# First batch of the attention projected, split and stored during the last scans; mask rows made by GpSimd at the start

## What is computed

```python
x = _layernorm(x + _L0_attn_ref(x, ...))       # state-space layer with a scan over positions
x = _layernorm(x + _L0_xattn_ref(x, ctx_2048, mask, mask, Wq, bq, Wk, bk, Wv, bv))
x = _layernorm(x + _L0_ffn_ref(x, w_gate_up, w_down))

# in _L0_xattn_ref: 16 heads of 16 channels; 512 queries and 512 keys for each of 16 batches
q = einsum('oc,bct->bot', Wq, target) + bq     # k and v likewise, from ctx
dot = einsum('bhdt,bhds->bhts', q, k) / sqrt(16)
m = mask_t * mask_s
dot = m * dot - (1.0 - m) * 1e6
out = einsum('bhts,bhds->bhdt', softmax(dot) * m, v)
```

## Time and profile before

| | us |
|---|---|
| median of 3 runs (lowest, highest) | 3583.75 (3581.31, 3584.29) |
| the profiled execution | 3582.23 |
| its span, first to last instruction | 3580.4 |

### The profile page before, as it was taken

The page is one execution under the profiler, slowest core; times in us unless marked ns, Lnnn a source line. Parts: engine busy times, 40 slices in busy tenths (PEclk is TensorE's granted clock), DMA queues, the critical chain, the costliest instruction groups (busy, mean ns, idle before and its releaser), DMA issues. The chain is left out here.

```text
span 3580.4 us, 53813 instructions
## 1 busy us (share of the span) xinstructions
PE 3088.7 (86%) x16101; PEld 1821.8 (51%) x16134; DVE 2916.8 (81%) x2901; ACT 2561.1 (72%) x4966; POOL 2256.2 (63%) x1409
## 2 busy tenths in 40 slices
PE   8788888888888888898887479899899899969998
PEld 5566656656666666566655233343343343324444
DVE  6999989989989989889999477677777777548886
ACT  6888877878878778788876137566666666757776
POOL 4999999989999999999999224233333334300000
PEclk9999999999999999999998689999999999989999
DMA  4102210210122022202210445554554555231110
GB/s 156 59 8 74 72 57 23 74 69 25 56 74 70 7 75 71 69 11 74 72 57 27 119 141 152 158 162 149 163 165 146 163 167 149 73 114 48 41 47 33
DMA packets 163681, 310.68 MB, mean 87 GB/s; under 512 B 22544, under 2 KB 80016, under 8 KB 163296
## 3 DMA queue, kind: packets, MB, share of 16 engines
q1 hardware_dynamic: 159088, 299.46, 26.4%
q10 hardware_dynamic: 4352, 8.39, 0.9%
HBM read 216.11 MB, written 91.69 MB: 86 GB/s over the span
## 5 line engine op out<-in xcount | busy, mean ns | idle before, releaser
L737 POOL TENSOR_TENSOR bu<-du,bc 128x1024 f32<-128x1024 f32 x512 | 1196.7, 2362 | 90.6 <-DVE dt L329 45.1
L810 DVE TENSOR_TENSOR_SCAN states<-states,bu 128x1024 f32<-128x1024 f32 x448 | 1026.6, 2292 | 118.5 <-ACT states L662 73.8
L662 ACT ACTIVATE states<-dt,negA 128x256 f32<-128x256 f32 x2048 | 851.0, 462 | 356.8 <-DVE hc L823 307.2
L1460 DVE TENSOR_REDUCE mmax<-s_ps 128x2 f32<-128x1024 f32 x512 | 624.8, 1224 | 285.0 <-PE s_ps L1180 270.8
L1296 ACT ACTIVATE pt<-s_ps 128x512 f32<-128x512 f32 x1024 | 572.7, 596 | 319.2 <-PE s_ps L1189 308.0
L484 PE MATMUL y_ps<-id_sb,hc 128*128 128x128 f32 x3584 | 485.9, 280 | 156.4 <-DVE hc L823 156.3
L823 DVE TENSOR_TENSOR hc<-states,bc 128x1024 f32<-128x1024 f32 x448 | 548.6, 1225 | 47.0 <-DVE states L810 1.9
L484 PEld LDWEIGHTS y_ps<-id_sb,hc 128*128 128x128 f32 x3584 | 410.7, 143 | 320.1 <-DVE hc L823 282.8
L1189 PE MATMUL s_ps<-qst,kst 105*128 105x512 bf16 x1024 | 380.6, 387 | 11.7 <-ACT pt L1296 5.1
L1180 PE MATMUL s_ps<-kst,qst 102*128 102x512 bf16 x1024 | 319.4, 395 | 54.7 <-DMA kst<-mask_d 44.8
L1200 PE MATMUL pv_ps<-pt,vaug 128*32 128x512 f32 x2048 | 278.4, 617 | 41.6 <-ACT o_sb L1331 41.5
(11 more groups left out here) (172 smaller groups left out, 4722.3 us busy)
## 6 DMA issues: line engine op xcount, KB each, us to landing
bc<-bc_scratch SPq DMA_DIRECT2D x128, 512.0 KB, 5.2
stack_d<-parts SPq DMA_DIRECT2D x192, 256.0 KB, 3.0
qst<-stack_d SPq DMA_DIRECT2D x64, 384.0 KB
kst<-stack_d SPq DMA_DIRECT2D x64, 384.0 KB
x<-xres SPq DMA_DIRECT2D x31, 512.0 KB, 6.2
w_raw<-in_w_ffn SPq DMA_DIRECT2D x48, 256.0 KB, 2.7
w_raw<-in_w_ffn SPq DMA_DIRECT2D x16, 768.0 KB, 6.8
xT_sb<-in_xT SPq DMA_DIRECT2D x16, 512.0 KB, 3.6
```

Source lines behind the costliest of these rows:

```text
L662: a = act.activation(states[:, bank, first:first + SEQ], dt[:, t, :], ACT.Exp, scale=negA[:, t, c * NS + n:c * NS + n + 1])
L737: pool.tensor_tensor(bu[:, buf, :].rearrange("p (n l) -> p n l", n=NS), du[:, t % (2 * GRP):t % (2 * GRP) + 1, :].to_broadcast([P, NS, SEQ ...
L810: m = dve.tensor_tensor_scan(dst, src, bu[:, BU_OF[k][0], half * 2 * SEQ:(half + n) * 2 * SEQ], 0.0, ALU.mult, ALU.add)
L1460: dve.tensor_reduce(mmax[:, u // HG, c:c + 2], s1_ps[:, pair], AX.X, ALU.max).then_inc(s1_free, 1)
```

## The change

The projections, split and stores of the attention's batch 0 move into the first stage's last batch (batch 15). SyncE loads their inputs, 1.79 MB in six DMAs, into tiles that the last batch no longer needs (`load_first_rows`, in batch 14 between the B and the C rows of batch 15). ACT takes the normalisation's sums (step 6) and scales (step 10), POOL its power (step 12); PE projects in steps 9, 11, 13 and 15, DVE masks in steps 10, 12, 14 and 16, ACT rounds in steps 15, 19, 19 and 23, POOL subtracts in steps 18, 21, 22 and 25; SyncE stores behind its loop (`store_first_rows`). One half output projection moves from step 14 to step 18, since it uses the bank. The mask rows are made by POOL at the program's start and stored before the first B and C rows. The second stage begins with body -1. SyncE issues only the loads of `qst`, `kst`, x and the mask there; ACT issues those of the parameters; the preset of `kst` is cut in two, and only its first half is waited for ahead of the first scores. Counts of semaphores are shifted by one batch to match; those lines are left out.

```diff
-            14: ((0, 0, 0, 2), (0, 1, 0, 2)), 20: ((0, 0, 2, 4), (0, 1, 2, 4)), 30: ((0, 0, 4, 6), (0, 1, 4, 6))}
+            14: ((0, 1, 0, 2),), 18: ((0, 0, 0, 2),), 20: ((0, 0, 2, 4), (0, 1, 2, 4)), 30: ((0, 0, 4, 6), (0, 1, 4, 6))}
 LAST_ADD = {7: 0, 11: 1}
+
+
+ROWS_AT = {("k", 0): (9, 10), ("k", 1): (11, 12), ("q", 0): (13, 14), ("q", 1): (15, 16)}
+NORM_AT, NORM_POW, NORM_END = 6, 12, 10
+CAST_AT = {("k", 0): 15, ("k", 1): 19, ("q", 0): 19, ("q", 1): 23}
+REST_AT = {("k", 0): 18, ("k", 1): 22, ("q", 0): 21, ("q", 1): 25}
...
+        a_wk, a_wq = [in_w(i * HID, HID).rearrange("p (k o) -> p k o", k=SEQT) for i in range(2)]
+        a_ctx, a_x, a_d, a_n, a_kf, a_qf = [in_w((i + 1) * 2 * HID, 2 * HID).rearrange("p (k t) -> p k t", k=SEQT) for i in range(6)]
+        a_m, a_m4 = [in_w(14 * HID + i * HID, HID) for i in range(2)]
...
+            sp.dma_start(mk, mask).then_inc(mk_in, 16)
...
+            sp.wait_ge(mk_ready, 1)
+            sp.dma_start(mask_d.rearrange("(b k) -> b k", b=BATCH), mk_rows.rearrange("b o r t -> b (o r t)")).then_inc(mk_out, 16)
...
+            def load_first_rows():
+                for kind in "scg":
+                    sp.wait_ge(mm[kind], BATCH * PER[kind])
+                sp.dma_start(a_x, x1[0].rearrange("(i p) h -> p i h", p=P)).then_inc(a_x_in, 16)
+                first = ctxt[0:SEQ * HID].rearrange("(i p h) -> p i h", p=P, h=HID)
+                for dst, src in ((a_ctx, first), (a_wk, wk), (a_wq, wq), (a_qkb, chan_qk), (a_m, mask[0:1, :].partition_broadcast(P))):
+                    sp.dma_start(dst, src).then_inc(a_in, 16)
+
+            def store_first_rows():
+                sp.wait_ge(a_norm, 1)
+                sp.dma_start(x1n_d[0:SEQ * HID].rearrange("(i p h) -> p i h", p=P, h=HID), a_n).then_inc(a_out, 16)
+                for opnd, kind in ((1, "k"), (0, "q")):
+                    sp.wait_ge(a_rest[kind], 2)
+                    for r, pair in enumerate(PAIRS):
+                        dst = stack_d[opnd, :, r * HDIM:(r + 1) * HDIM].rearrange("m r h t -> (r h) m t")
+                        sp.dma_start(dst, a_parts[kind][:, pair[opnd]]).then_inc(a_out, 16)
...
+                    if b == BATCH - 2:
+                        load_first_rows()
...
+            store_first_rows()
             sp.wait_ge(w_sc_ready, 2)
...
+                    elif lo == 0 and i == 0:
+                        pe.wait_ge(a_ev, len(ROWS_AT))
                     elif lo == 0:
                         pe.wait_ge(ev["o"], seq("o", b - 1, i))
                     unit(1 + i, "o", i, b + off, par if off == 0 else 1 - par, lo, hi)
+
+            def first_rows(kind, i):
+
+                bank = proj_banks[:, 1, :]
+                if (kind, i) == ("k", 0):
+                    pe.wait_ge(a_in, 5 * 16)
+                    pe.wait_ge(ev["o"], seq("o", BATCH - 2, 0))
+                else:
+                    pe.wait_ge(a_ev, list(ROWS_AT).index((kind, i)))
+                if (kind, i) == ("q", 0):
+                    pe.wait_ge(a_norm, 1)
+                w, src = (a_wk, a_ctx) if kind == "k" else (a_wq, a_n)
+                for half in range(2):
+                    cols = slice(half * (HID // 2), (half + 1) * (HID // 2))
+                    for k in range(SEQT):
+                        m = pe.matmul(bank[:, cols], w[:, k, i * P:(i + 1) * P], src[:, k, cols], start=(k == 0), stop=(k == SEQT - 1))
+                m.then_inc(a_mm, 1)
...
+                        for (kind, i), (at, _) in ROWS_AT.items():
+                            if at == k:
+                                first_rows(kind, i)
...
+            def norm_first():
+                act.wait_ge(a_x_in, 16)
+                for i in range(SEQT):
+                    act.activation(a_d[:, i], a_x[:, i], ACT.Copy, accum_out=a_sum[:, i:i + 1])
+                act.drain()
+                act.activation(a_mean, a_sum, ACT.Copy, scale=-1.0 / HID)
+                act.drain()
+                for i in range(SEQT):
+                    act.activation(a_d[:, i], a_x[:, i], ACT.Identity, bias=a_mean[:, i:i + 1])
+                act.drain()
+                for i in range(SEQT):
+                    act.activation(a_x[:, i], a_d[:, i], ACT.Square, accum_out=a_sq[:, i:i + 1])
+                act.drain()
+                act.activation(a_ve, a_sq, ACT.Copy, bias=EPS, scale=1.0 / HID).then_inc(a_stats, 1)
+                act.wait_ge(a_in, 5 * 16)
+                act.activation(a_m4, a_m, ACT.Copy, scale=HDIM ** -0.5)
+
+            def scale_first():
+                act.wait_ge(a_stats, 2)
+                for i in range(SEQT):
+                    m = act.activation(a_n[:, i], a_d[:, i], ACT.Identity, scale=a_rs[:, i:i + 1])
+                m.then_inc(a_norm, 1)
+
+            def cast_first(kind, i):
+                if i == 0:
+                    act.wait_ge(a_ev, 2 if kind == "k" else 4)
+                else:
+                    act.wait_ge(a_rest[kind], 1)
+                act.activation(a_parts[kind][:, i], a_kf if kind == "k" else a_qf, ACT.Copy).then_inc(a_cast[kind], 1)
...
+            pool.wait_ge(mk_in, 16)
+            pool.tensor_scalar(mk_n, mk, 1.0, NEG, ALU.subtract, ALU.mult)
+            for side, part in enumerate((mk, mk_n)):
+                at = [[pair[side] for pair in PAIRS].index(i) for i in range(3)]
+                pool.drain()
+                pool.tensor_copy(mk_rows[:, side, at[0], :], part)
+                pool.drain()
+                pool.tensor_tensor(mk_r, part, mk_rows[:, side, at[0], :], ALU.subtract)
+                pool.drain()
+                pool.tensor_copy(mk_rows[:, side, at[1], :], mk_r)
+                pool.drain()
+                pool.tensor_tensor(mk_rows[:, side, at[2], :], mk_r, mk_rows[:, side, at[1], :], ALU.subtract)
+                pool.drain()
+                for r, pair in enumerate(PAIRS):
+                    if r not in at:
+                        pool.tensor_copy(mk_rows[:, side, r, :], mk_rows[:, side, at[pair[side]], :])
             pool.drain()
+            pool.engine_nop().then_inc(mk_ready, 1)
...
+            def last_rows(k):
+                if k == NORM_POW:
+                    pool.wait_ge(a_stats, 1)
+                    pool.memset(a_half, -0.5)
+                    pool.drain()
+                    pool.tensor_tensor(a_rs, a_ve, a_half, ALU.pow).then_inc(a_stats, 1)
+                for (kind, i), at in REST_AT.items():
+                    if at == k:
+                        x, parts = a_kf if kind == "k" else a_qf, a_parts[kind]
+                        pool.wait_ge(a_cast[kind], i + 1)
+                        dst = x if i == 0 else parts[:, 2]
+                        pool.tensor_tensor(dst, x, parts[:, i], ALU.subtract).then_inc(a_rest[kind], 1)
...
+                dst, factor, col = (a_kf, a_m, 1) if kind == "k" else (a_qf, a_m4, 0)
+                dve.wait_ge(a_mm, list(ROWS_AT).index((kind, i)) + 1)
+                if kind == "q":
+                    dve.wait_ge(a_norm, 1)
+                dve.scalar_tensor_tensor(dst[:, i, :], proj_banks[:, 1, :], a_qkb[:, col, i:i + 1], factor,
+                                         ALU.add, ALU.mult).then_inc(a_ev, 1)
...
-            for b in (-2, -1, 0):
+            for b in (-1, 0):
...
-            load_x1(0)
-            load_mask(0)
-            sp.wait_ge(mask_rows, 1)
-            sp.dma_start(mask_d.rearrange("(b k) -> b k", b=BATCH), mk_rows.rearrange("b o r t -> b (o r t)")).then_inc(mask_out, 16)
-            sp.wait_ge(mask_out, 16)
+            load_group(0, 0, 0, (0,))
+            load_group(0, 0, 1, (0,))
+            load_x1(1)
+            sp.wait_ge(preset, 1)
+            for g in range(2):
+                load_group(0, 0, g, (1,))
+            load_mask(1)
+            for g in range(2, HGROUPS):
+                load_group(0, 0, g)
...
+            load_ctx(1, 1)
+            for dst, src in ((wk_sb, wk), (wq_sb, wq), (qkb, chan_qk)):
+                act.dma_start(dst.ap(), src).then_inc(kq_params, 16)
             load_ctx(0, 0)
+            for dst, src in ((id2, ident), (wv_sb, wv), (w_sc, w_scales)):
+                act.dma_start(dst.ap(), src).then_inc(params, 16)
+            act.dma_start(bv_sb[:, :], bv.partition_broadcast(P)).then_inc(params, 16)
...
-            pool.memset(kst.ap().rearrange("p a h t -> p (a h t)").bitcast(F32), MINUS_ONES).then_inc(preset, 1)
+            pool.memset(kst[:, 0].rearrange("p h t -> p (h t)").bitcast(F32), MINUS_ONES).then_inc(preset, 1)
+            pool.memset(kst[:, 1].rearrange("p h t -> p (h t)").bitcast(F32), MINUS_ONES).then_inc(preset, 1)
...
-            dve.tensor_scalar(mk_n, mk, 1.0, NEG, ALU.subtract, ALU.mult)
-            for side, x in enumerate((mk, mk_n)):
-                at = [[pair[side] for pair in PAIRS].index(part) for part in range(3)]
-                dve.drain()
-                three_parts(dve, [mk_rows[:, side, r, :] for r in at], x, mk_r)
-                dve.drain()
```

(30 more changed lines are left out.)

138 lines of the change are left out of this document (83 added, 55 removed).

## The result

| kernel | median us (lowest, highest) | runs |
|---|---|---|
| before | 3584.02 (3581.31, 3585.89) | 4 |
| changed | 3537.90 (3524.35, 3541.99) | 4 |

The ratio is 0.9865, 95% interval 0.9838 to 0.9893: 46 us faster where 28 were forecast, and outside the range of 3544 to 3568. The profiled execution of the changed kernel took 3541.99 us, so 40.2 less than that of before.

The account below looks back on a forecast made before the run. DVE and POOL were at their limit in the last batch, while one chain left engines mostly idle for 54.5 us at the hand-over. -41.0 + 8.3 + 5.3 = -27.4 from 3582.23 gives 3554.8, as median 3556; range 3544 to 3568.

Parts of the forecast that it names:

- hand-over: Second stage's start to first score product: 54.5 us shrinks to 13.5, a gain of 41.0, between 39 and 46.
- last batch: First stage's last batch: the added projections, maskings and normalisation cost 8.3 us, between 3.0 and 16.
- front: Program's start: POOL's mask rows beside DVE cost 5, between bounds 0 and 10.4, plus 0.3 for a DMA issue: 5.3 us.
- attention from the first score on: Second stage: body -1 as before, 44.4 us; another time in the attention's loop would make the forecast wrong.
- even share: Second stage's first loads: both queues share evenly, 3.5 MB before the last operand, 12.0 + 2.2 = 14.2 us.
- step 1, C rows: Last batch: six loads of 1.79 MB ahead of the C rows delay DVE by 1.0 us (0 to 2.6).
- step 10, DVE waits for PE: Last batch: DVE waits 3.4 us for PE's projection, plus 0.75 for the masking: 4.1 us.
- steps 12 to 20, three maskings (and ACT): Last batch, steps 12, 14, 16: three maskings of 2.25 us, less 0.9 of former idling for POOL: 1.4.
- steps 23 and 24, GpSimd: Last batch: POOL gets 9.5 us more work, and its lateness leads DVE's by 1 to 2: 1.3 us.
- A: Rival at the program's start: DVE and POOL exclude each other in full, 5.4 us more, 3562 us; chance 0.27.
- B: Rival: mask rows at the program's start cost nothing, the last batch's added work only 5 to 6, 3548 us; chance 0.15.
- rivals A to D: Besides A and B: C, operands late or PE's clock low, 3569 us, chance 0.10; D, last batch in lockstep, 3597, 0.03.

Follow-up runs that it names:

- Experiment 4: Changed kernel with the first stage's loop over batch pairs written out instead of looped: on all engines 3501.3 us, on DVE alone 3532.7 us.

## Why the prediction was wrong, step by step

| step of the prediction | forecast | in the profile |
|---|---|---|
| hand-over | -41.0 | -39.9 |
| last batch | +8.3 | +10.4 |
| front | +5.3 | +6.9 |
| batches 0 to 14 | 0 | +4.3 |
| attention from the first score on | 0 | -21.8 |
| sum | -27.4 | -40.0 |

**Hand-over: right.** The first score product came 14.8 us after the stage's start (13.5 forecast, near the even share; the queues moved 256 GB/s, not 289), and body -1 was as long as before. Between these ends the gain is 39.7 us (54.5 - 14.8); the table's 39.9 is read from the last sum and not from the stage's start. Two blemishes cost nothing here: the lower end, 6.1 + 1.2 + 1, is 8.3 and not 8.5, and of its 1.2 and 1 us the rows show only the sum, as 7.7 - 5.2 = 2.5 us at before's first projection.

**Last batch: right in its mechanism, 2.1 short.** How much later each scan starts than in before gives the size of each term, in us:

| term | forecast | measured |
|---|---|---|
| step 1, C rows | 1.0 | 2.1 |
| steps 7 to 9, ACT | 0.5 | 0.6 |
| step 10, DVE waits for PE | 4.1 | 4.5 |
| steps 12 to 20, three maskings (and ACT) | 1.4 | 0.3 |
| steps 23 and 24, GpSimd | 1.3 | 2.0 |
| tail, last y sums | none | 0.9 |

```profile
1891.44 1.22 DVE L981 TENSOR_TENSOR hc<-states,bc 128x1024 f32<-128x1024 f32 x1 [2.60 <-DMA bc<-bc_scratch]
...
1929.89 0.75 DVE L1013 SCALAR_TENSOR_TENSOR win_sb<-proj,diagW,win_sb 128x512 f32<-128x512 f32 x1 [3.98 <-PE proj L617]
```

The C rows were the most mis-sized term: DVE waited 2.60 us for them where before it had 0.48. At step 10 it waited 3.98 for PE (forecast 3.4). The other three maskings had no wait, and waits of 0.84 and 0.79 us for GpSimd at steps 13 and 20 were gone, so they were too dear by 1.1. GpSimd led at steps 23 and 24 with 0.66 and 1.14. DVE's wait for the last y sums grew from 1.5 to 2.7 and stood in no term. DVE's waits for the decays grew from 0.8 to 2.8 in all, but the one at step 7 only took the place of one for GpSimd (1.02 before). That the sum is no further off is partly luck, since the maskings' 1.1 hid as much of the rest.

**Front: right that neither bound holds, 1.6 short.** First bu at 52.9, where the forecast had 51, A 56.5 and B 46.3. The 5 us were picked between two bounds, so that they come near is luck in part; and the mask rows took GpSimd 13.9 us and not 11.5. The Trainium skill's "SBUF — State Buffer", section "Who interferes with whom", is right that the two engines disturb each other, for scalings and for products of two SBUF tiles. Its full exclusion, rival A, is not what happened: DVE lost 7.8 us beside 14 us of GpSimd's work, and while GpSimd's first instruction ran (5.85 to 7.81), DVE began and ended four scalings in 1.22 us.

**The failed step** is a term put at nothing without a reason: that the attention's loop takes the time it took. It gave 21.8 us in the profile. The prediction named it as the thing that would make it wrong and gave it neither a price nor a chance. I had read what is in the loop, which had hardly changed, and not where its code lies. 20 instructions more of ACT ahead of the loop took away five fetches of 6.3 to 6.7 us, 32.4 in all. On before such a shift is worth 31 us (3585.0 to 3554.4), on the changed kernel 28 to 35 (3563.9 and 3567.7 against 3532.5 and 3536.1). With the place held equal, the change itself brings 18 to 22 us with the loop in a bad place (3585.5 against 3567.7 and 3563.9) and as much in a good one (3554.4 against 3536.1 and 3532.5), which is also the 18.3 at the first score product. That is 5 to 10 under the forecast: the front, the last batch, the hand-over and the 4.3 of the batches between. With the attention as long as before, the time would have come near 3564, inside the range; what put it outside was the attention.

**Batches 0 to 14.** 1.5 of the 4.3 come in batch 0, where DVE waits 3.8 us for y sums and not 2.3. The rest comes at the jumps back: from 400 to 1700 us DVE's first scans wait 25.8 us in five (16.2 put to issue, 9.6 to GpSimd) against 21.4. Experiment 4 shows that these waits go with the jump back. That they are late fetches is argued from the packets there and from the attention's loop; the place of the first stage's loop was not shifted. Why they are each 1 us longer in the changed kernel was not tested.

**Open.** What varies between executions of the changed kernel (18 us over its first four runs) is not settled. In all good places the first loop bodies still take 62 to 71 us, with PE waiting up to 6.7 us for kst, and the later ones 62 to 66. In the slow bodies of the changed kernel ACT's load of ctx is issued 0 to 1.4 us behind SyncE's first load of qst, in the others 2.7; that the one causes the other was not tried. Nor is it settled why the loss of 32.4 us of stops shortened the attention by only 21.8 us in this profile, and by 25.2 and 30.7 in two others without stops (1020.4 and 1014.9 for 1045.6). The rivals A to D did not come about; the last batch never fell into lockstep.

## What to carry to other kernels

A hardware loop has a place as well as a length. Before a small change is priced, look at the jumps back: an idle time put to "issue" on the first instruction of a turn, together with packets on the instruction queue all through the loop, was a fetch here, and its cost came and went with 20 to 64 instructions ahead of the loop on that engine. When two kernels are compared, hold that place equal, or the edit is credited with it.

## What the runs showed of the hardware

- ACT's loop of 337 to 339 instructions was fetched anew at each jump back from four of the places tried and not from three; the piece that fits is 128 instructions (8192 bytes on queue 14), three of them kept. One such stop took 6.3 to 7.4 us here. In the 6 us ahead of a stop's end the DMA engines were busy throughout (share 1.04, 264 GB/s from 2438 to 2444 us in before); whether that makes the fetch so long was not tried.
- GpSimd on 16 partitions slowed DVE on 128: four scalings from 0.87 to 2.12 us, three products of SBUF tiles from 1.60 to 3.39 us.
- Writing the first stage's loop out six times, 4968 instructions on ACT instead of 2536, left no stop at those places; the medians fell by 31 to 37 us, 27 of which the profile shows ahead of the attention.
